# Next block's x_proj, softplus and turned u two states earlier, and z ahead of its block in a second buffer

## The chip, the cores and the metric

The kernel runs on one core of a Trainium2 chip. The metric is the device time of one execution in microseconds (us), as the median of repeated runs. The engines are TensorE (PE; its weight loads are shown as PEld), VectorE (DVE), ScalarE (ACT), GpSimd (POOL) and SyncE (SP, which issues the DMAs). Each works through its own queue in order, and semaphores tie the queues together.

## The reference, cut to what matters

The program is four layers behind one another: a selective state space layer, a mixture of experts, a linear attention with a feed-forward part, and two layers of windowed attention. Only the first is touched. It computes, for `x` of 4 x 1024 x 256 that has been layer-normalised:

```python
xz = einsum('bld,ed->ble', x, W_in);  u, z = split(xz, 2)     # 512 channels each
uc = silu(depthwise_conv3(u) + conv_b)
x_dbl = einsum('blh,eh->ble', uc, W_xproj)                    # 96 columns: dt 64, B 16, C 16
dt = softplus(einsum('blr,hr->blh', dtp, W_dt) + b_dt)
A = -exp(A_log)                                               # 16 states
def step(h, inp):                                             # over time
    h = exp(dt_t * A) * h + B_t * u_t                         # 16 states x 512 channels
    y_t = einsum('bn,bnh->bh', C_t, h)
y = (ys + D * uc) * silu(z)
out = x + einsum('blh,dh->bld', y, W_out)
```

All arithmetic is in float32.

## The kernel before, in words

`state_space_stage` cuts the 4096 tokens into N = 8 blocks of 512 (two to a sequence) and goes over NS = 16 states in each. One iteration `i` stands for one state of one block: block k = i // 16, state i % 16. Every engine has the same loop over `i` from FIRST = -20 to END, and each step of a block's preparation and of its closing is put at a fixed offset r = i - 16 k from the block's first state. So r = -12 is state 4 of the block before, r = -1 is its state 15, and the order on each engine is written out by hand. In the prologue (negative i) the first block's preparation runs with no scans beside it.

What one state takes, with the names that the profile shows:

- GpSimd `scale_u(i)` (L322): four instructions, u turned to time-major (`uT`) times the state's column of B (in `bcT`), into `ub`. `add_odd` (L336): two sums into `acc`.
- TensorE `inject` (L830): turns `ub` back to channel-major in the four banks `pu`, 16 transposes. `transpose_state` (L842): turns the scanned state of the iteration before into `pt`, 16 transposes.
- ScalarE `step_decay` (L450): exp(dt * A) into `da`, in two instructions. `weigh` (L462): two multiplications of turned states by C.
- VectorE `scan` (L620): four scans, one for each 128 channels. `add_even` (L630): two sums into `acc`.

In TensorE's queue the transposes and injections of a state stand in the order T0 T1, I0, I1, T2 T3, I2, I3, and `first_product` and `second_product`, each in two parts, put the matmuls of other blocks between them. They all use the two PSUM banks `pf`, one after the other, so every user waits for the one before.

The preparation of block k before the change, by r:

- r = -17 normalisation on ScalarE (`normalised`, L472); -19 its statistics on VectorE (L535); -18 `norm_factors` on GpSimd
- r = -12, -11 `product_u` (L687); -11, -10 `convolve` (L563) on VectorE
- r = -8 Silu of `uc` on ScalarE (L485), at the end of the iteration
- r = -6 `product_xd` (x_proj, L712), -5 to -3 `product_dt` (L734) and `magnitude` (L385, L386), -3 Exp (L488), -2 Ln (L491), -1 the sum `dt` = relu + ln on VectorE (L591, after the second scan)
- r = -3 to -1 `transpose_u` (L743) and `turn_u` (L380), which make `uT`
- r = 6, 7 `product_z` (L700) and `copy_z`; r = 8 Silu of `z` (L494)
- r = 18 to 20 `transpose_sum` (L763) and `gate` (L570); 24, 25 `product_out` (L774); 25, 26 `output` (L576)

Both Silus fall into iteration 8 of a block (z of this block, `uc` of the next), with a table load before them and one back to the Exp and Ln set behind (L521).

At the turn to the next block the order is another one. On GpSimd `scale_u` of state 0 is issued in iteration 15, not 14, and of state 1 behind the sums. On ScalarE `step_decay` of state 0 stands behind `first_product`. On TensorE all of state 0's injections stand behind `transpose_state` and `second_product` of iteration 15. `scale_u` of state 0 waits for all four `turn_u` of its block, the last of which is at r = -1. `begin_sum` (L328, four instructions, `skip` times `uT`) starts the next block's sums at r = -1 and 0.

Of the kernel before, what the change touches and what calls it, by code (L numbers as in the profile page):

```python
# [162 lines left out]
def state_space_stage(nc, tag, w, src, dst, ident):  # L163
# [6 lines left out]
    with ExitStack() as ctx:  # L170
# [17 lines left out]
        z = s.sb("z", [P, CT, BLK])  # L188
# [51 lines left out]
        FIRST, END = -20, NS * N + 11  # L240
# [51 lines left out]
        def _(pool):  # L292
# [46 lines left out]
            for i in range(FIRST, END):  # L339
                turn_ends = (i + 1) % NS == 0  # L340
                if turn_ends and 0 <= i + 1 < N * NS:
                    scale_u(i + 1)
                if not turn_ends and (i + 2) % NS and 0 <= i + 2 < N * NS:
                    scale_u(i + 2)
# [3 lines left out]
                if turn_ends and 0 <= i + 2 < N * NS:  # L348
                    scale_u(i + 2)
# [13 lines left out]
        def _(act):  # L363
            give_credit(act, weighed)

            def copy_z(k, c):
                act.wait_ge(z_made.sem, z_made.at(k, c + 1))
                nc.scalar.activation(z[:, c, :], pf[c % 2][:, :], ACT.Copy).then_inc(z_copied.sem, 1)
# [40 lines left out]
            def first_product(i):  # L409
                for k in range(N):  # L410
# [5 lines left out]
                    elif r in (-12, -11):  # L416
                        copy_u(k, 2 * (r + 12))
                    elif r in (-5, -4, -3):
                        magnitude(k, (0, 1, 3)[r + 5])
                    elif r in (-2, -1):  # L420
                        turn_u(k, 2 * r + 5)
                    elif r in (6, 7):
                        copy_z(k, 2 * (r - 6))

            def second_product(i):
                for k in range(N):
# [5 lines left out]
                    elif r in (-12, -11):  # L432
                        copy_u(k, 2 * (r + 12) + 1)
                    elif r == -6:
                        projected(k)
                    elif r == -5:
                        bc_columns(k)
                    elif r == -4:
                        magnitude(k, 2)
                    elif r in (-3, -2):  # L440
                        turn_u(k, 2 * (r + 3))
                    elif r in (6, 7):
                        copy_z(k, 2 * (r - 6) + 1)
# [32 lines left out]
            def rest_of_step(i):  # L476
                for k in range(N):
# [5 lines left out]
                    elif r == -8:  # L483
                        act.wait_ge(conv_steps.sem, conv_steps.at(k))
                        nc.scalar.activation(uc[:, :, :], uc[:, :, :], ACT.Silu).then_inc(uc_ready.sem, 1)  # L485
                    elif r == -3:
                        act.wait_ge(abs_ready.sem, abs_ready.at(k))
                        nc.scalar.activation(work[:, :, :], work[:, :, :], ACT.Exp, scale=-1.0).then_inc(soft_steps.sem, 1)  # L488
                    elif r == -2:
                        act.wait_ge(soft_steps.sem, soft_steps.at(k, 1))  # L490
                        nc.scalar.activation(work[:, :, :], work[:, :, :], ACT.Ln, bias=1.0).then_inc(soft_steps.sem, 1)  # L491
                    elif r == 8:
                        act.wait_ge(z_copied.sem, z_copied.at(k))
                        nc.scalar.activation(z[:, :, :], z[:, :, :], ACT.Silu).then_inc(z_ready.sem, 1)  # L494

            for i in range(FIRST, END):
# [9 lines left out]
                if (i + 1) % NS and 0 <= i + 1 < N * NS:  # L506
# [4 lines left out]
                if (i + 1) % NS and 0 <= i + 1 < N * NS:  # L511
# [12 lines left out]
        def _(dve):  # L524
# [41 lines left out]
            def gate(k, c):  # L566
# [3 lines left out]
                nc.vector.tensor_tensor(gatedT[:, c, :], pf[c % 2][:, :], z[:, c, :], ALU.mult).then_inc(gated_ready.sem, 1)  # L570
# [8 lines left out]
            def after_second_scan(i):  # L579
                for k in range(N):  # L580
# [3 lines left out]
                    elif r == 26:  # L584
# [3 lines left out]
                    elif r == -1:  # L588
# [5 lines left out]
            def rest_of_step(i):  # L594
                for k in range(N):
# [9 lines left out]
                    elif r == 25:  # L605
# [44 lines left out]
        def _(pe):  # L650
            give_credit(pe, bu_made, state_turned, turned_made)

            def transpose_hidden(k, d):
                if d == 0:
                    pe.wait_ge(h0_ready.sem, h0_ready.at(k))
                if k:
                    pe.wait_ge(uT_ready.sem, uT_ready.at(k - 1, 4 - d))
# [47 lines left out]
            def product_xd(k, c):  # L705
                if c == 0:
# [3 lines left out]
                    elif k:  # L710
                        pe.wait_ge(z_copied.sem, z_copied.at(0, 3))
# [4 lines left out]
            def transpose_bc(k):  # L716
# [3 lines left out]
                elif k:  # L720
                    pe.wait_ge(z_copied.sem, z_copied.at(0))
# [24 lines left out]
            def transpose_sum(k, c):  # L746
# [7 lines left out]
                elif k == N - 2:  # L754
                    pe.wait_ge(uT_ready.sem, uT_ready.at(k + 1, 4 - c))
# [10 lines left out]
            def product_out(k, half, t, part):  # L766
                if t == 0 and part == 0:
                    if half == 0:
                        pe.wait_ge(gated_ready.sem, gated_ready.at(k))
                    if k + 1 < N:  # L770
                        pe.wait_ge(z_copied.sem, z_copied.at(k + 1, 3 + half))
# [1740 lines left out]
```

## Time and profile before

| | us |
|---|---|
| median of 3 runs | 3998.52 |
| the runs | 3998.52, 3992.69, 4001.32 |
| the profiled execution's time | 3997.76 |
| its span, first to last instruction | 3995.9 |
| first scan starts, last scan ends | 66.3, 1020.2 |
| mean granted TensorE clock, share of full | 0.961 |

The scans of the state space stage take 953.9 of the 3995.9 us; what follows them is not edited. A step below is the time from the first scan of one state to the first scan of the next. In an even block a step in which VectorE never waits and has nothing else to do takes 5.76 us, in an odd block 6.00, since there the scans take a carry.

### The profile page before, as it was taken

To read this page: it belongs to the slowest core of one execution; us is meant where nothing else is said; L and a number is where in the kernel's file an instruction comes from. 1 tells how busy PE (TensorE), PEld (TensorE's weight loads), DVE (VectorE), ACT (ScalarE), POOL (GpSimd) and SP (SyncE) were. 2 spreads that over 40 slices of the span, in tenths; PEclk is the share of its full clock that TensorE was granted. 3 is DMA by queue.
4 is the path that set the end of the run, shared out by engine and by line. 5 is a ranking of instruction groups with operands and counts; after the bars stand their busy time and mean duration, and the time that the engine had idled before them with its cause. 6 is when DMAs were issued, how large, how long until landed. Compare 5 with 4: busy or idle time off the path is not lost. (4 is left out here: it accounts for less than half of the span.)

```text
span 3995.9 us, 59179 instructions
## 1 busy us (share of the span) xinstructions
PE 3643.4 (91%) x21704; PEld 2593.4 (65%) x21704; DVE 2522.0 (63%) x5386; ACT 1601.5 (40%) x3052; POOL 1392.0 (35%) x1567
## 2 busy tenths in 40 slices
PE   6888878887799999999998998999979989999799
PEld 3666666666455688888886664666645556666465
DVE  4898988899566455555554444777743357777333
ACT  5666666666100122222221213666631146666211
POOL 4778777788100000000000223444411134444111
PEclk8899999999899999999998998999989999999899
DMA  1000000000200100000001112111122011111221
GB/s 39 1 11 12 1 11 11 11 6 6 87 32 32 35 12 12 12 12 12 11 11 55 64 63 64 38 34 37 38 63 64 27 59 33 38 34 34 74 64 37
DMA packets 150197, 129.32 MB, mean 32 GB/s; under 512 B 20804, under 2 KB 147544, under 8 KB 149656
## 3 DMA queue, kind: packets, MB, share of 16 engines
q1 hardware_dynamic: 149912, 125.54, 10.0%
q8 instruction: 177, 2.90, 0.3%
q14 instruction: 108, 0.88, 0.1%
HBM read 87.73 MB, written 37.77 MB: 31 GB/s over the span
## 5 line engine op out<-in xcount | busy, mean ns | idle before, releaser
L830 PEld LDWEIGHTS ssm_pu<-ident,ssm_ub 128*128 128x128 f32 x2048 | 255.8, 150 | 220.3 <-issue 86.0
L830 PE MATMUL ssm_pu<-ident,ssm_ub 128*128 128x128 f32 x2048 | 325.4, 292 | 80.4 <-POOL ssm_ub L322 47.2
L322 POOL TENSOR_SCALAR ssm_ub<-ssm_uT,ssm_bcT 128x512 f32<-128x512 f32 x512 | 356.4, 718 | 96.7 <-ACT ssm_uT L380 63.4
L336 POOL TENSOR_TENSOR ssm_acc<-ssm_acc,ssm_weighted 128x512 f32<-128x512 f32 x256 | 328.4, 1292 | 143.4 <-ACT ssm_weighted L462 143.0
L842 PE MATMUL ssm_pt<-ident,ssm_state 128*128 128x128 f32 x2048 | 288.5, 285 | 82.6 <-DVE ssm_acc L630 58.6
L2256 PE MATMUL win_pa<-win_w_wqkv,win_hT 128*128 128x512 f32 x768 | 357.9, 603 | 1.6 <-ACT win_hT L2043 1.1
L620 DVE TENSOR_TENSOR_SCAN ssm_state<-ssm_da,ssm_carry,ssm_pu 128x512 f32<-128x512 f32 x256 | 312.2, 1260 | 21.2 <-PE ssm_pu L830 16.4
L1838 PE MATMUL glu_up<-glu_hT,glu_w_w 128*128 128x512 f32 x704 | 309.4, 599 | 3.4 <-DVE glu_hT L1761 3.4
L620 DVE TENSOR_TENSOR_SCAN ssm_state<-ssm_da,ssm_pu 128x512 f32<-128x512 f32 x256 | 296.6, 1199 | 25.1 <-PE ssm_pu L830 16.9
L842 PEld LDWEIGHTS ssm_pt<-ident,ssm_state 128*128 128x128 f32 x2048 | 240.4, 147 | 107.9 <-DVE ssm_acc L630 67.8
L2017 POOL TENSOR_TENSOR win_rotated<-win_straight,win_turned 128x512 f32<-128x512 f32 x128 | 163.0, 1274 | 417.0 <-DVE win_turned L2132 417.0
L462 ACT ACTIVATE ssm_weighted<-ssm_pt,ssm_bcT 128x512 f32<-128x512 f32 x256 | 175.7, 686 | 319.6 <-PE ssm_pt L842 273.0
L2063 ACT ACTIVATE win_probs<-win_sc,win_nbias,win_rn 128x256 f32<-128x256 f32 x512 | 281.9, 560 | 28.9 <-DVE win_nbias L2160 21.9
L450 ACT ACTIVATE ssm_da<-ssm_dt,ssm_decay 128x1024 f32<-128x1024 f32 x256 | 292.7, 1147 | 1.4 <-DVE ssm_dt L591 1.4
L2155 DVE CUSTOM_DVE_ANT_0 win_sc<-win_sc,win_c_masks 128x256 f32<-128x256 f32 x512 | 205.7, 444 | 118.2 <-PE win_sc L2273 118.2
L1273 POOL TENSOR_TENSOR lin_rstd<-lin_mv,lin_eps 128x1 f32<-128x1 f32 x32 | 6.1, 190 | 718.2 <-DVE lin_mv L142 718.2
L1473 PE MATMUL lin_pa<-lin_hT,lin_wqk 128*128 128x128 f32 x2048 | 245.7, 278 | 3.7 <-DVE lin_hT L1362 0.8
L1838 PEld LDWEIGHTS glu_up<-glu_hT,glu_w_w 128*128 128x128 f32 x704 | 135.3, 193 | 168.3 <-issue 162.4
L1473 PEld LDWEIGHTS lin_pa<-lin_hT,lin_wqk 128*128 128x128 f32 x2048 | 233.5, 192 | 13.7 <-DVE lin_qkT L1372 8.9
L1774 DVE SCALAR_TENSOR_TENSOR glu_act<-glu_up,glu_w_b,glu_gel 128x512 f32<-128x512 f32 x96 | 71.9, 749 | 252.8 <-ACT glu_gel L1731 236.6
L1117 PE MATMUL moe_ex<-moe_w_experts,moe_hT 128*128 128x512 f32 x512 | 226.0, 594 | 0.0
L2256 PEld LDWEIGHTS win_pa<-win_w_wqkv,win_hT 128*128 128x128 f32 x768 | 138.6, 194 | 131.6 <-issue 129.7
(241 smaller groups left out, 7295.3 us busy)
## 6 DMA issues: line engine op xcount, KB each, us to landing
win_raw<-in_tables SPq DMA_DIRECT2D x64, 128.0 KB, 2.2
a<-win_y SPq DMA_DIRECT2D x64, 128.0 KB, 1.7
glu_xs<-a SPq DMA_DIRECT2D x32, 256.0 KB, 3.3
glu_x<-a SPq DMA_DIRECT2D x16, 512.0 KB, 5.3
ssm_x<-in_L_attn_x SPq DMA_DIRECT2D x8, 512.0 KB, 3.9
x<-ssm_out SPq DMA_DIRECT2D x16, 256.0 KB, 2.1
moe_x<-x SPq DMA_DIRECT2D x8, 512.0 KB, 3.9
x<-moe_y SPq DMA_DIRECT2D x8, 512.0 KB, 2.9
```

Of the source, the lines that this page charges most:

```text
L322: nc.gpsimd.tensor_scalar(ub[:, i % 2, t, :], uT[:, k % 2, t, :], bcT[:, k % 2, t, n:n + 1], 1.0, ALU.mult, ALU.mult).then_inc(ub_ready.se ...
L336: nc.gpsimd.tensor_tensor(acc[:, k % 2, t, :], acc[:, k % 2, t, :], weighted[:, j, :], ALU.add)\
L450: nc.scalar.activation(da[:, i % 2, pairs[p], :], dt[:, k % 2, pairs[p], :], ACT.Exp, scale=decay[:, n:n + 1]).then_inc(da_ready.sem, 1)
L620: nc.vector.tensor_tensor_scan(state[:, i % 2, c, :], da[:, i % 2, c, :], pu[c][:, :], carry[:, n, c:c + 1] if k % 2 else 0.0, ALU.mult, A ...
L830: last = nc.tensor.transpose(pu[c][:, t * P:(t + 1) * P], ub[:, i % 2, t, c * P:(c + 1) * P], ident)
L842: last = nc.tensor.transpose(pt[t % 2][:, c * P:(c + 1) * P], state[:, i % 2, c, t * P:(t + 1) * P], ident)
L1117: last = nc.tensor.matmul(ex[pair][:, :], hT[:, turn.side, k, t * P:(t + 1) * P], experts[:, k, pair * 2 * D:(pair + 1) * 2 * D], start=(k ...
L1473: last = nc.tensor.matmul(pa[g % 2][:, r * P:(r + 1) * P], wqk[:, g // 2, k, cols], hT[:, k, :], start=(k == 0), stop=(k == KD - 1))
L1838: last = nc.tensor.matmul(bank[:, :], w1[:, k, at:at + P], hT[:, k, :], start=(k == 0), stop=(k == KD - 1))
L2063: nc.scalar.activation(probs[:, head, :], sc[j][:, r, :], ACT.Exp, bias=nbias[:, g, j, r:r + 1], scale=rn[:, turn.side, 0, head:head + 1], ...
L2155: return nc.vector.tensor_tensor_reduce(sc[j][:, r, :], sc[j][:, r, :], mask, 1.0, -3e38, ALU.add, ALU.max, highest[:, g, j, r:r + 1])
L2256: last = nc.tensor.matmul(bank[:, :], hT[:, k, :], wqkv[:, k, g * INNER:(g + 1) * INNER], start=(k == 0), stop=(k == KD - 1))
```

## The change

The preparation from x_proj to the sum of dt and the turned u moves from r = -6 ... -1 to r = -8 ... -3. The Silu of `uc` moves from -8 to -9 and that of `z` from 8 to 7, so that both are in iteration 7, and x_proj is in the iteration right behind. `product_z` and `copy_z` move from r = 6, 7 to r = -2, -1, that is into iterations 14 and 15 of the block before, for which `z` gets a second buffer. `product_out` and `output` move two iterations up. The special order at the turn is taken out on GpSimd, ScalarE and TensorE: state 0 of a block is treated as any other. The waits on the banks `pf` follow the new order. No instruction is added or dropped, and none of the DMAs is edited.

```diff
-        z = s.sb("z", [P, CT, BLK])
+        z = s.sb("z", [P, 2, CT, BLK])
-        FIRST, END = -20, NS * N + 11
+        FIRST, END = -20, NS * N + 9
@@ GpSimd, main loop @@
-                turn_ends = (i + 1) % NS == 0
-                if turn_ends and 0 <= i + 1 < N * NS:
-                    scale_u(i + 1)
-                if not turn_ends and (i + 2) % NS and 0 <= i + 2 < N * NS:
+                if 0 <= i + 2 < N * NS:
                     scale_u(i + 2)
                 if 0 <= i - 1 < N * NS:
                     add_odd(i - 1, 0)
                     add_odd(i - 1, 1)
-                if turn_ends and 0 <= i + 2 < N * NS:
-                    scale_u(i + 2)
@@ ScalarE, first_product @@
-                    elif r in (-5, -4, -3):
-                        magnitude(k, (0, 1, 3)[r + 5])
+                    elif r in (-7, -6, -5):
+                        magnitude(k, (0, 1, 3)[r + 7])
+                    elif r in (-4, -3):
+                        turn_u(k, 2 * r + 9)
                     elif r in (-2, -1):
-                        turn_u(k, 2 * r + 5)
-                    elif r in (6, 7):
-                        copy_z(k, 2 * (r - 6))
+                        copy_z(k, 2 * (r + 2))
@@ ScalarE, rest_of_step: Silu of uc, Exp, Ln, Silu of z @@
-                    elif r == -8:
+                    elif r == -9:
...
-                    elif r == -3:
+                    elif r == -5:
...
-                    elif r == -2:
+                    elif r == -4:
...
-                    elif r == 8:
+                    elif r == 7:
@@ ScalarE, main loop @@
                 first_product(i)
-                if (i + 1) % NS == 0 and 0 <= i + 1 < N * NS:
-                    step_decay(i + 1, 0)
-                    step_decay(i + 1, 1)
                 rest_of_step(i)
-                if i % NS == NS // 2:
+                if i % NS == NS // 2 - 1:
                     nc.scalar.preload_act_table_set("natural_log_exp_and_others")
@@ VectorE: output, half 1; the sum of dt; output, half 0 @@
-                    elif r == 26:
+                    elif r == 24:
...
-                    elif r == -1:
+                    elif r == -3:
...
-                    elif r == 25:
+                    elif r == 23:
@@ TensorE, product_z, the bank that it waits for @@
-                    elif k + 1 < N:
-                        pe.wait_ge(u_copied.sem, u_copied.at(k + 1, c + 3))
                     else:
-                        pe.wait_ge(gated_ready.sem, gated_ready.at(k - 1, c + 3))
+                        pe.wait_ge(uT_ready.sem, uT_ready.at(k, 4 - c))
@@ TensorE, first_product; second_product alike @@
-                    elif r == -6:
+                    elif r == -8:
                         product_xd(k, part)
-                    elif r in (-5, -4, -3) and part:
-                        product_dt(k, (0, 1, 3)[r + 5])
-                    elif r in (-2, -1) and part == 0:
-                        transpose_u(k, 2 * r + 5)
-                    elif r in (6, 7):
-                        product_z(k, 2 * (r - 6), part)
+                    elif r in (-7, -6, -5) and part:
+                        product_dt(k, (0, 1, 3)[r + 7])
+                    elif r in (-4, -3) and part == 0:
+                        transpose_u(k, 2 * r + 9)
+                    elif r in (-2, -1):
+                        product_z(k, 2 * (r + 2), part)
                     elif r in (18, 19) and part:
                         transpose_sum(k, 2 * (r - 18))
-                    elif r in (24, 25):
-                        product_out(k, 0, r - 24, part)
+                    elif r in (22, 23):
+                        product_out(k, 0, r - 22, part)
@@ TensorE, main loop @@
                 first_product(i, 0)
-                if ahead and not turn_ends:
+                if ahead:
                     inject(i + 1, 0)
...
                 second_product(i, 0)
-                if ahead and turn_ends:
-                    inject(i + 1, 0)
-                    inject(i + 1, 1)
                 if ahead:
                     inject(i + 1, 2)
```

## Rows read from the trace of the kernel before

**Rows 1.** Windows by block: length, busy PE, PEld, DVE, ACT, POOL, clock, DMA

```profile
304.76:426.82 122.06, 100.44 (x638) 78.17 (x637) 108.84 (x123) 82.95 (x119) 93.73 (x106) 0.93 0.03 10
...
sum 953.86, PE 787.64 PEld 612.59 DVE 866.33 ACT 634.07 POOL 735.10; mean PE 98.46 PEld 76.57 DVE 108.29 ACT 79.26 POOL 91.89
```

**Rows 2.** Windows by stage: blocks 1 and 2, steps 0-2, 8-11, 12-14, 15

```profile
180.34:201.94 21.60, 20.22 (x143) 19.20 (x142) 18.94 (x19) 12.31 (x19) 21.60 (x25) 0.81 0.00 1
...
241.43:272.36 30.93, 27.79 (x172) 22.26 (x170) 25.92 (x27) 19.98 (x22) 22.16 (x25) 0.94 0.11 34
...
292.18:304.77 12.59, 4.84 (x28) 4.08 (x27) 8.29 (x9) 7.70 (x12) 5.96 (x11) 0.72 0.00 1
304.77:326.42 21.65, 17.53 (x123) 16.20 (x122) 18.21 (x20) 11.55 (x18) 21.65 (x25) 0.85 0.00 1
...
364.63:395.28 30.65, 27.41 (x178) 21.79 (x176) 25.17 (x27) 21.66 (x28) 23.12 (x25) 1.00 0.11 35
395.28:414.76 19.48, 17.14 (x123) 13.36 (x122) 19.34 (x30) 18.80 (x29) 13.83 (x15) 1.00 0.01 1
414.76:426.80 12.04, 4.41 (x28) 3.67 (x27) 8.04 (x9) 7.79 (x13) 6.07 (x11) 0.74 0.00 0
```

**Rows 3.** Timeline of the turn from block 1 to block 2: start, length, instruction

```profile
291.51 1.91 ACT L491 ACTIVATE ssm_work<-ssm_work 128x2048 f32<-128x2048 f32 x1
...
294.54 2.27 DVE L591 TENSOR_TENSOR ssm_dt<-ssm_dt,ssm_work 128x2048 f32<-128x2048 f32 x1
...
297.52 1.93 PE L842 MATMUL ssm_pt<-ident,ssm_state 128*128 128x128 f32 x8 [3.61 <-DVE ssm_acc L630]
...
300.07 0.59 ACT L380 ACTIVATE ssm_uT<-ssm_pf 128x512 f32<-128x512 f32 x1
...
300.76 2.70 POOL L322 TENSOR_SCALAR ssm_ub<-ssm_uT,ssm_bcT 128x512 f32<-128x512 f32 x4 [6.55 <-ACT ssm_uT L380]
...
304.77 1.22 DVE L620 TENSOR_TENSOR_SCAN ssm_state<-ssm_da,ssm_pu 128x512 f32<-128x512 f32 x1 [4.30 <-PE ssm_pu L830]
```

**Rows 4.** Timeline of TensorE in steps 7 and 8 of block 2

```profile
359.65 1.04 PE L842 MATMUL ssm_pt<-ident,ssm_state 128*128 128x128 f32 x8
...
361.83 1.02 PE L700 MATMUL ssm_pf<-ssm_hT,ssm_w_in 128*128 128x512 f32 x2
...
363.12 1.04 PE L842 MATMUL ssm_pt<-ident,ssm_state 128*128 128x128 f32 x8
...
366.59 1.04 PE L842 MATMUL ssm_pt<-ident,ssm_state 128*128 128x128 f32 x8
```

**Rows 5.** Timeline around the two Silus, step 9 of block 2

```profile
371.14 0.69 ACT L462 ACTIVATE ssm_weighted<-ssm_pt,ssm_bcT 128x512 f32<-128x512 f32 x1 [1.27 <-PE ssm_pt L842]
...
374.96 1.90 ACT L485 ACTIVATE ssm_uc<-ssm_uc 128x2048 f32<-128x2048 f32 x1
...
376.88 1.28 ACT L521 ACT_TABLE_LOAD   x1
...
380.04 0.66 PE L842 MATMUL ssm_pt<-ident,ssm_state 128*128 128x128 f32 x4 [2.42 <-ACT ssm_weighted L462]
```

**Rows 6.** Two lines of VectorE during the scans: ns min/median/max

```profile
L563 DVE SCALAR_TENSOR_TENSOR ssm_uc<-ssm_u,ssm_conv_w,ssm_uc x56: 721/853/4276, 96.0 to 849.8; 128x512 f32<-128x512 f32 x56
...
L591 DVE TENSOR_TENSOR ssm_dt<-ssm_dt,ssm_work x8: 2254/2263/2293, 60.1 to 907.5; 128x2048 f32<-128x2048 f32 x8
```

**Rows 7.** Timeline of GpSimd and VectorE, step 5 of block 0

```profile
95.83 2.70 POOL L322 TENSOR_SCALAR ssm_ub<-ssm_uT,ssm_bcT 128x512 f32<-128x512 f32 x4
96.03 5.06 DVE L563 SCALAR_TENSOR_TENSOR ssm_uc<-ssm_u,ssm_conv_w,ssm_uc 128x512 f32<-128x512 f32 x2
...
98.48 1.27 POOL L336 TENSOR_TENSOR ssm_acc<-ssm_acc,ssm_weighted 128x512 f32<-128x512 f32 x1
```

**Rows 8.** Timeline ahead of the first scan

```profile
65.04 3.25 PE L830 MATMUL ssm_pu<-ident,ssm_ub 128*128 128x128 f32 x14 [5.21 <-POOL ssm_ub L322]
```

**Rows 9.** Window around the end of the prologue, columns as in rows 1

```profile
51.85:68.92 17.07, 10.08 (x36) 7.38 (x37) 4.92 (x4) 14.44 (x19) 7.75 (x10) 0.50 0.00 1
```

More of the change, by code:

```diff
@@ L433, in second_product @@
                         copy_u(k, 2 * (r + 12) + 1)
+                    elif r == -8:
+                        projected(k)
+                    elif r == -7:
+                        bc_columns(k)
                     elif r == -6:
[L435 to L438, printed above, removed]
                         magnitude(k, 2)
-                    elif r in (-3, -2):
-                        turn_u(k, 2 * (r + 3))
-                    elif r in (6, 7):
-                        copy_z(k, 2 * (r - 6) + 1)
+                    elif r in (-5, -4):
+                        turn_u(k, 2 * (r + 5))
+                    elif r in (-2, -1):
+                        copy_z(k, 2 * (r + 2) + 1)
             def step_decay(i, p):
@@ L505, in _ @@
                     carry_over(i - 1)
-                if (i + 1) % NS and 0 <= i + 1 < N * NS:
+                if 0 <= i + 1 < N * NS:
                     step_decay(i + 1, 0)
@@ L510, in _ @@
                 second_product(i - 1)
-                if (i + 1) % NS and 0 <= i + 1 < N * NS:
+                if 0 <= i + 1 < N * NS:
                     step_decay(i + 1, 1)
@@ L656, in transpose_hidden @@
                 if k:
-                    pe.wait_ge(uT_ready.sem, uT_ready.at(k - 1, 4 - d))
+                    pe.wait_ge(z_copied.sem, z_copied.at(k - 1, 3 + d))
                 for t in range(TB):
@@ L719, in transpose_bc @@
                     pe.wait_ge(out_ready.sem, out_ready.at(k - 2))
-                elif k:
-                    pe.wait_ge(z_copied.sem, z_copied.at(0))
                 for t in range(TB):
@@ L754, in transpose_sum @@
                 elif k == N - 2:
-                    pe.wait_ge(uT_ready.sem, uT_ready.at(k + 1, 4 - c))
+                    pe.wait_ge(z_copied.sem, z_copied.at(k + 1, 3 + c))
                 elif k % 2:
@@ L769, in product_out @@
                         pe.wait_ge(gated_ready.sem, gated_ready.at(k))
-                    if k + 1 < N:
-                        pe.wait_ge(z_copied.sem, z_copied.at(k + 1, 3 + half))
+                    if k + 2 < N:
+                        pe.wait_ge(u_copied.sem, u_copied.at(k + 2, 3 + half))
                 first = (2 * half + t) * P
@@ L809, in second_product @@
                         product_u(k, 2 * (r + 12) + 1, part)
-                    elif r == -6:
+                    elif r == -8:
                         product_xd(k, 2 + part)
-                    elif r == -5 and part == 0:
+                    elif r == -7 and part == 0:
                         transpose_bc(k)
-                    elif r == -4 and part == 0:
+                    elif r == -6 and part == 0:
                         product_dt(k, 2)
-                    elif r in (-3, -2) and part == 0:
-                        transpose_u(k, 2 * (r + 3))
-                    elif r in (6, 7):
-                        product_z(k, 2 * (r - 6) + 1, part)
+                    elif r in (-5, -4) and part == 0:
+                        transpose_u(k, 2 * (r + 5))
+                    elif r in (-2, -1):
+                        product_z(k, 2 * (r + 2) + 1, part)
                     elif r in (18, 19) and part == 0:
                         transpose_sum(k, 2 * (r - 18) + 1)
-                    elif r in (24, 25):
-                        product_out(k, 1, r - 24, part)
+                    elif r in (22, 23):
+                        product_out(k, 1, r - 22, part)
             def inject(i, c):
@@ L847, in _ @@
                     pe.wait_ge(w_in_loaded, 16)
-                elif i == -6:
+                elif i == -8:
                     pe.wait_ge(weights, 16 * 8)
@@ L853, in _ @@
                     transpose_state(i - 1, 1)
-                turn_ends = i % NS == NS - 1
                 first_product(i, 0)
-                if ahead and not turn_ends:
+                if ahead:
                     inject(i + 1, 0)
                 first_product(i, 1)
-                if ahead and not turn_ends:
+                if ahead:
                     inject(i + 1, 1)
```

11 lines of the change are left out of this document (5 added, 6 removed).

## The prediction

> **What bounds the kernel now.** I read the windows by block first. The eight blocks of scans take 953.9 us, of which VectorE is busy 866.3; GpSimd has 735.1 [rows 1]. VectorE sets the pace, and the stage can win no more than its idle 87.5 us. The reader should hold every edit against that number.
>
> Then the windows by stage, to see where that idle time lies [rows 2]. In steps 12 to 14 of block 2 there is next to none (19.48 - 19.34 = 0.14); in step 15, the turn, 12.04 - 8.04 = 4.00, and 12.59 - 8.29 = 4.30 in block 1. In steps 0 to 2 it is 2.66 and 3.44. In steps 8 to 11 it is 5.01 and 5.48. These three places are 12.0 and 12.9 us a block; seven times their mean is 87 us, which is nearly all of it.
>
> Third, the timeline of the turn [rows 3]. VectorE does the sum of dt at 294.54, so TensorE, which needs `add_even` behind it, stands 3.61 us. The last quarter of turned u is copied at 300.07, GpSimd starts `scale_u` of state 0 at 300.76 after 6.55 us idle and needs 2.70, and only then can the injection begin and VectorE scan at 304.77, after 4.30 us. TensorE runs at 1.2 GHz from this hole on: eight transposes take 1.93 us at 297.52 against 1.04 at full clock [rows 3, 4].
>
> **The turn, step 15.** The change takes the chain turned u, `scale_u`, injection off the path: uT is complete in iteration 13, `scale_u` of state 0 is issued in 14, and its 2.70 us end some 4 us before the injection in 15. The 4.15 us (mean of the two blocks) go. What comes in their place:
>
> *Sum of dt in step 13.* Its VectorE time moves at no cost in itself. But it needs the Ln. Before, the Ln ended at 291.51 + 1.91 = 293.42 and the sum began at 294.54, so 1.1 us of slack [rows 3]; that slack rests on the statistics of step 13 (steps 12 to 14 of block 2 are 19.48 us against 3 x 5.76 = 17.28, so 2.2), which lay between Exp and Ln and now come behind the sum. So VectorE waits about 2.2 - 1.1 = 1.1 us. Also, GpSimd was waiting for turned u when this sum ran at the turns, and it took 2254 to 2293 ns [rows 6]. Now it has `scale_u` and `add_odd` beside it. What that can cost shows in the convolution, likewise two SBUF inputs on VectorE: 721 ns at best, 853 in the median, 4276 at worst [rows 6], the worst when it began 0.2 us behind a `scale_u` [rows 7]. So 0.1 to 3.5 us, in part under the wait for Ln. I take 1.3 for Ln and GpSimd together.
>
> The Trainium skill (SBUF — State Buffer, Who interferes with whom) says that a VectorE instruction with two SBUF inputs and a GpSimd instruction that reads SBUF exclude each other for a whole instruction, and whichever comes second is blocked. By that rule the wait would end with the GpSimd instruction in progress; rows 7 show a wait longer than any one instruction there, so the rule agrees in kind, and the sum goes by the rows.
>
> *z in steps 14 and 15.* In steps 7 and 8 z's matmuls and the output's stand between the transposes, and one state takes TensorE 366.59 - 359.65 = 6.94 us. Two z matmuls and four transposes take 363.12 - 361.83 = 1.29, so a z matmul 0.43 and eight in a step 3.44 [rows 4]. Steps 14 and 15 so want 6.94 us of TensorE against 5.76 or 6.00 of VectorE. One z pair (0.86) fits in the hole that step 13 leaves; the rest makes TensorE about 2 us late at the end of step 15, where it has roughly 2.3 before VectorE's `add_even` waits, and step 0, with only eight extra transposes, gives it back. I take 0.3. At nothing or 2.4 us lie the bounds.
>
> *Clock.* Step 13 now holds the sum and the statistics, so TensorE stands some 3.5 and then 1.5 us. After such holes the clock was 0.72 and 0.74 of full over the turn [rows 2]. If a quarter of the 6.94 us of step 14 runs at 1.2 GHz, 1.7 us of TensorE are lost, part of it in time in which it waits anyway: I take 0.7 (0 to 3.5, which is half of the step).
>
> Turn afterwards: 1.3 + 0.3 + 0.7 = 2.3. Saved 4.15 - 2.3 = 1.85, seven times: **13 us**.
>
> **Steps 0 to 2.** Mean idle 3.05 us. GpSimd is busy in all of their 21.60 and 21.65 us [rows 2]: it starts the block late (idle 6.55 at the turn, [rows 3]) and has four instructions of `begin_sum` on top. The lateness goes, `begin_sum` stays: four of 1.27 like L336 [rows 7], so 5.1 us over steps 15 and 0. A plain step is 2.70 + 2 x 1.27 = 5.24 us of GpSimd, so it regains 0.5 a step, and its lead is about 4 us (`scale_u` may begin some 7 us before it is wanted, and needs 2.70). I leave 1.4 us of waiting; saved 1.6, but less in blocks whose idle time there is shorter: seven times 1.45, **10 us** (0 to 17).
>
> **Steps 7 to 11.** Two effects of opposite sign. z leaves steps 6 and 7 and the output takes its place, so 6.94-us steps end at step 8 instead of 10. But x_proj now stands right behind the Silus. In block 2: the second transposes of step 7 end at 364.0 [rows 4], the weighting (0.69, [rows 5]) by 364.9; table load and both Silus fill the time from the weighting's end, 371.83, to 376.86 = 5.0 us [rows 5], so `uc` is ready at 369.9. TensorE is at x_proj at 366.59 + 0.87 = 367.5 [rows 4] and stands 2.4 us. Queued behind are injections of state 9 and T2, T3 of state 7; with two pairs of x_proj and two injections before them (2.6 us) T2 is done at about 373.2. VectorE, which now has an output in each of steps 7 and 8, wants it at about 371.3: 2.0 us idle. T3 needs the weighting, which after a Silu comes 380.04 - 376.86 = 3.2 us later [rows 5], about the same time. By the same walk smaller waits follow for T0 of state 8 (0.8) and for the dt products, which wait for the xd copy as before (0.8). With 0.8 for a slow stretch of clock that makes 4.4 in an even block. In an odd block each step is 0.24 longer and TensorE a microsecond less late, so the same sum gives 2.5. Mean over four even and three odd: 3.6. Saved 5.25 - 3.6 = 1.6, seven times: **11 us** (-15 to 20).
>
> **Prologue.** Here z comes without cover: 16 matmuls after the last turned u, which TensorE has done 5.21 us before 65.04, so they begin at 60 to 61; ten of them stand ahead of the first injection [rows 8]. The clock is at half in this stretch [rows 9], so a matmul takes 0.86 and ten 8.6 us: the injection begins near 69.4. At full clock it would begin near 65.4. Near the slow end, since the stretch before is slow: **4 us lost** (0.4 to 7). In the tail nothing changes: only empty iterations go. The output's and the x loads' DMAs leave two steps earlier; no wait of VectorE names a load during the scans, so nothing.
>
> **Sum.** 13 + 10 + 11 - 4 = 30 us. The profiled execution took 3997.8, within 0.02% of the median 3998.5: 3997.8 - 30 = **3968 us**.
>
> **The rivals.**
>
> *A. The clock eats the turn.* The double hole of step 13 leaves TensorE at 1.2 GHz for all of step 14, when it has most to do. Each turn then loses half of 6.94 us, less what it waits anyway: 3.3 in place of 0.7, and 30 - 7 x 2.6 = 12 us are saved, **3986 us**. For it: two holes there as now. Against: the second is shorter, since the injections of step 13 lie between.
>
> *B. No change.* GpSimd takes VectorE's place around the turn. From step 14 to 2 it has 5 x 5.24 + 5.1 = 31.3 us of its own, and the sum of dt blocks it 2.3 more, against some 29.5 of VectorE. Then the 10 us of steps 0 to 2 don't come and 1.9 more a turn is lost: 30 - 10 - 13 = 7, **3991 us**, within 0.2% (8 us) of before, which is about what a measurement here can tell. Against: over a block GpSimd is busy 93.7 of 122.1 us, so it catches up [rows 1].
>
> *C. Slower: x_proj behind the Silus.* If the burst on ScalarE begins half a step (2.9 us) later than reckoned, TensorE stands 5.3 us at x_proj, and after so long a hole half of a 6.94-us step at 1.2 GHz costs 3.5 in place of my 0.8. That is 5.6 more in each of seven blocks and 3 in the prologue: 42 us, **4010 us**. It decides from some 4.3 us a block beyond my 3.6. Against: T2 and T3 of step 7 bound the burst's start, and they are early.
>
> *D. More.* Ln in time, no slow clock: turn 1.0, steps 7 to 11 at 2.5: 9 + 8 us more, **3951 us**.
>
> **How the numbers follow.** Forecast 0.56, D 0.14, A 0.15, B 0.08, C 0.07. The forecast's own range is 3957 to 3980. To hold 8 in 10 the range takes in D and A and leaves B and C: 3948 to 3989. Faster by over 0.2% (below 3990.5): the forecast, D, nearly all of A: 0.85. Within 0.2%: B and a little of A: 0.08. Slower: C, 0.07.
>
> **What would show it.** Right: blocks of 116 to 119 us instead of 122 to 124; no VectorE wait for `pu` at the turn, `scale_u` of state 0 over before step 15; step 13 of 10 us and more, with L591 over 2.3 us where it meets GpSimd; a TensorE wait of 2 to 3 us for L485 at L712; first scan near 70. Wrong: a wait for L712 over 4 us, step 14 or 15 over 8 us at half clock, or L336 holding L462 in steps 0 to 2 as before.

## The result, and the profile after

The changed kernel takes **3943.04 us** (median of 4 runs, 3941.39 to 3943.43) beside 3998.18 (4 runs) for the kernel before: a ratio of 0.9863, 95% interval 0.9846 to 0.988. It is 55 us faster, where 30 were forecast; the time lies 5 us under the low end of the range, 3948. The profiled execution has a span of 3941.6 us (3995.9 before), and its scans take 896.9 us (953.9 before).

Windows by block of the changed kernel (blocks 0 to 2, then the sum over all eight), columns as in [rows 1]:

```profile
68.51:179.54 111.03, 93.42 (x580) 69.67 (x579) 104.27 (x114) 81.72 (x117) 93.77 (x104) 0.94 0.00 1
179.54:295.48 115.94, 100.31 (x657) 76.15 (x656) 111.81 (x121) 82.01 (x108) 96.83 (x107) 0.99 0.03 10
295.48:408.74 113.26, 98.18 (x637) 75.79 (x636) 108.53 (x123) 82.45 (x118) 95.55 (x105) 0.97 0.03 10
...
sum 896.95, PE 770.09 PEld 590.55 DVE 863.75 ACT 633.07 POOL 752.29; mean PE 96.26 PEld 73.82 DVE 107.97 ACT 79.13 POOL 94.04
```

Blocks 1 to 5 are 113.2 to 116.0 us long instead of the 116 to 119 that I expected. VectorE's idle time in the scans, 87.5 us before [rows 1], is 33.2. GpSimd's busy time is longer by 17 us (752.3 against 735.1) in scans that are shorter by 57. Two rows of VectorE's waits from 66 to 960 us (us in total, times, longest), the first of the kernel before, the second of the changed one, show the chain that left the turn; the one wait that stays is the first scan's:

```profile
DVE ssm_state L620 <- PE ssm_pu L830: 33.2, 8, 4.5
```

```profile
DVE ssm_state L612 <- PE ssm_pu L816: 4.2, 1, 4.2
```

Windows by stage (block 1: steps 0-2; block 2: steps 0-2, 12-14, 15, and behind these steps 13 and 14 by themselves), columns as in [rows 2]:

```profile
179.54:198.51 18.97, 18.16 (x145) 15.56 (x144) 18.70 (x20) 15.61 (x26) 18.96 (x22) 1.00 0.01 1
...
295.48:313.45 17.97, 15.74 (x124) 13.23 (x123) 17.97 (x20) 14.45 (x24) 17.97 (x20) 1.00 0.01 1
...
379.97:402.98 23.01, 17.90 (x118) 14.16 (x116) 21.87 (x30) 17.91 (x26) 18.52 (x19) 0.93 0.00 1
402.98:408.74 5.76, 5.76 (x36) 4.14 (x35) 5.76 (x7) 3.34 (x5) 5.68 (x10) 1.00 0.01 3
...
385.73:397.24 11.51, 8.07 (x54) 7.12 (x53) 10.37 (x18) 8.92 (x14) 10.17 (x11) 0.85 0.00 1
397.24:402.98 5.74, 5.16 (x28) 3.15 (x27) 5.74 (x8) 3.23 (x6) 3.35 (x4) 1.00 0.00 0
```

The turn is now a plain step: 5.76 us with VectorE busy throughout, where it was 12.04 with 4.00 idle [rows 2]. Steps 0 to 2 went from 21.65 to 17.97 us with no idle time, though GpSimd is still busy in all of them. Steps 12 to 14 are longer, since the sum of dt lies there now; 1.14 us of idle time came with it. The granted clock was 0.72 over the turn to block 2 and 0.85 in its steps 0 to 2 before [rows 2]; now it is 1.00 in both, and 0.85 in step 13 of block 2.

The table has VectorE's idle time (length of a step less VectorE's busy time in it) over all eight blocks, by stage, in us; the kernels below the first two are the experiments.

| kernel | 0-2 | 3-6 | 7-11 | 12 | 13-14 | 15 | idle | busy | scans |
|---|---|---|---|---|---|---|---|---|---|
| before | 19.5 | 1.0 | 35.9 | 0 | 0.9 | 30.3 | 87.5 | 866.3 | 953.9 |
| **after** | 1.3 | 1.0 | 24.9 | 0 | 5.2 | 0.8 | 33.2 | 863.7 | 896.9 |
| turn_order_back | 13.5 | 1.0 | 23.6 | 0 | 5.3 | 6.2 | 49.6 | 867.3 | 916.9 |
| gpsimd_order_back | 19.3 | 1.0 | 26.1 | 0 | 5.4 | 18.8 | 70.6 | 870.3 | 940.9 |
| pe_act_order_back | 1.6 | 1.0 | 22.3 | 0 | 5.1 | 6.1 | 36.1 | 862.9 | 899.0 |
| before_no_begin | 5.2 | 1.0 | 36.0 | 0 | 0.9 | 28.8 | 71.8 | 863.6 | 935.4 |
| after_double_begin | 41.7 | 1.0 | 22.5 | 0 | 5.1 | 0.9 | 71.2 | 868.9 | 940.1 |
| stats_early | 3.0 | 1.0 | 23.9 | 0.9 | 1.1 | 3.8 | 33.7 | 862.4 | 896.2 |
| narrow_z | 4.4 | 1.0 | 25.9 | 0 | 5.1 | 0 | 36.5 | 866.2 | 902.7 |
| silu_uc_first | 2.3 | 1.0 | 17.3 | 0 | 5.2 | 0.9 | 26.6 | 863.3 | 889.9 |
| weigh_first | 1.3 | 1.0 | 24.4 | 0 | 5.1 | 0.9 | 32.7 | 863.8 | 896.5 |
| silu_and_weigh | 2.0 | 1.0 | 9.2 | 0 | 5.2 | 0.5 | 17.8 | 862.2 | 880.0 |
| all_three | 3.0 | 1.0 | 9.3 | 0.9 | 2.5 | 5.1 | 21.9 | 863.8 | 885.7 |

From before to after: steps 13 to 15 -25.2, steps 0 to 2 -18.1, steps 7 to 11 -11.0, VectorE's busy time -2.6, the start of the first scan +2.2 (68.51 against 66.3), after the last scan +0.4. Together -54.3, which is by what the spans differ.

Timeline of step 13 of block 2, the place to which the sum of dt moved, and of what follows (start, length, instruction):

```profile
387.07 1.94 ACT L486 ACTIVATE ssm_work<-ssm_work 128x2048 f32<-128x2048 f32 x1
...
388.06 4.74 POOL L322 TENSOR_SCALAR ssm_ub<-ssm_uT,ssm_bcT 128x512 f32<-128x512 f32 x4
...
389.04 2.52 DVE L583 TENSOR_TENSOR ssm_dt<-ssm_dt,ssm_work 128x2048 f32<-128x2048 f32 x1 [0.99 <-ACT ssm_work L486]
...
392.28 1.09 PE L828 MATMUL ssm_pt<-ident,ssm_state 128*128 128x128 f32 x8 [3.40 <-DVE ssm_acc L622]
...
395.42 1.70 PE L828 MATMUL ssm_pt<-ident,ssm_state 128*128 128x128 f32 x8
395.83 2.70 POOL L322 TENSOR_SCALAR ssm_ub<-ssm_uT,ssm_bcT 128x512 f32<-128x512 f32 x4 [0.38 <-PE ssm_pu L816]
```

Three things are to be seen. The sum waits 0.99 us for the Ln, as worked out (1.1). It runs beside `scale_u` and takes 2.52 us, only 0.25 more than before [rows 6]; the price fell on `scale_u`, 4.74 us instead of 2.70: one of its four instructions took 2.73 us, the others 0.70. At all seven turns it is so, and seven times 2.04 are 14 of the 17 us by which GpSimd's busy time grew (an estimate). And `scale_u` of the next block's state 0, the one at 395.83, is over at 398.5, some 10 us before that state's first scan at 408.74. TensorE stands 3.40 us behind the sum, does eight transposes at full clock (1.09 us) and then eight in 1.70 us, where 1.04 is the full clock and 1.93 the half one [rows 3, 4]. So the half clock came, but in step 13 (0.85) and not in step 14 (1.00), where I had put it, and VectorE has no idle time in steps 14 and 15.

### The profile page after: what moved, and what is told of

It reads as the page before. It is cut to its first block and busy times, and to the rows that moved or that the text cites. A ratio compares the mean times of both kernels' runs of the same rounds, so it can differ in the third digit from the quotient of the medians.

```text
span 3941.6 us, 59176 instructions
## 1 busy us (share of the span) xinstructions
PE 3632.8 (92%) x21704; PEld 2572.8 (65%) x21704; DVE 2520.7 (64%) x5386; ACT 1600.2 (41%) x3052; POOL 1410.5 (36%) x1567
## 5 line engine op out<-in xcount | busy, mean ns | idle before, releaser
L322 POOL TENSOR_SCALAR ssm_ub<-ssm_uT,ssm_bcT 128x512 f32<-128x512 f32 x512 | 371.7, 747 | 65.6 <-ACT ssm_uT L375 41.9
L816 PEld LDWEIGHTS ssm_pu<-ident,ssm_ub 128*128 128x128 f32 x2048 | 241.1, 144 | 183.0 <-issue 76.6
L816 PE MATMUL ssm_pu<-ident,ssm_ub 128*128 128x128 f32 x2048 | 315.2, 282 | 42.8 <-DVE ssm_state L612 29.0
```

The costliest lines, as they stand in the source:

```text
L322: nc.gpsimd.tensor_scalar(ub[:, i % 2, t, :], uT[:, k % 2, t, :], bcT[:, k % 2, t, n:n + 1], 1.0, ALU.mult, ALU.mult).then_inc(ub_ready.se ...
L816: last = nc.tensor.transpose(pu[c][:, t * P:(t + 1) * P], ub[:, i % 2, t, c * P:(c + 1) * P], ident)
```

## The experiments

All ratios are to the kernel before, run on the same chip, with 95% intervals. The medians are to be held against 3943.0 for the changed kernel. The kernel before had medians of 3995.6 to 3998.2 in the four sets of runs, so a difference of 2 or 3 us between medians of two sets says nothing.

### Which part of the turn matters

**turn_order_back**: the changed kernel with the old order at the turn on three engines.

```diff
@@ GpSimd @@
-                if 0 <= i + 2 < N * NS:
+                if turn_ends and 0 <= i + 1 < N * NS:
+                    scale_u(i + 1)
+                if not turn_ends and (i + 2) % NS and 0 <= i + 2 < N * NS:
                     scale_u(i + 2)
...
+                if turn_ends and 0 <= i + 2 < N * NS:
+                    scale_u(i + 2)
@@ ScalarE: step_decay of state 0 behind first_product @@
@@ TensorE: inject(i + 1, 0) and (i + 1, 1) behind second_product(i, 0) @@
```

> The changed kernel with the old order at the turn put back on GpSimd, ScalarE and TensorE: state 0's scale_u in iteration 15, its decay behind first_product, its injections behind T2, T3. Preparation and z stay early. Theory 1 (turned u was late; with it early, the order matters little): VectorE's idle time in step 15 is 1 us or less a turn instead of 0.1, the kernel 0 to 7 us slower than the changed one (3943). Theory 2 (the order itself held VectorE: state 0's injections wait behind T2, T3 and z): 2 to 4 us a turn come back in step 15 and some of the 2.8 us a block in steps 0 to 2, so 20 to 35 us slower, 3963 to 3978.

3965.26 us, 0.9919 [0.9905, 0.9934]. So 22 us of the 55 hang on the order, once the preparation is early, and the other 33 come without it. No run has the new order with the old preparation. Most of what comes back is not at the turn (6.2 against 0.8), where theory 2 had 2 to 4 us a turn, but in steps 0 to 2 (13.5 against 1.3). Of the 20 us by which the scans are longer, 3.6 are busy time of VectorE, nearly all of it in step 5 of block 0 (what happens there is told with narrow_z).

**gpsimd_order_back** and **pe_act_order_back**: the same edit in two halves, GpSimd's alone, and TensorE's with ScalarE's.

> The changed kernel with the old order at the turn on GpSimd alone: scale_u of state 0 in iteration 15, that of state 1 behind the sums. The whole old order came out 20 us of scans slower than the changed kernel (916.9 against 896.9 us), 12 of them as idle time in steps 0 to 2. Theory 1 (GpSimd's start an iteration late is what costs): 15 to 20 us slower than the changed kernel, with most of the idle time in steps 0 to 2. Theory 2 (the injections behind z and the transposes on TensorE cost): 5 us or less.

> The changed kernel with the old order at the turn on TensorE and ScalarE alone. Theory 1 (GpSimd's order costs): 3 to 6 us slower than the changed kernel, the 5.4 us of step 15, and little in steps 0 to 2. Theory 2 (TensorE's order costs): 15 to 20 us, as the whole old order.

GpSimd's half: 3986.01 us, 0.9974 [0.9964, 0.9984]. The other half: 3944.81 us, 0.987 [0.9857, 0.9884]. Windows over all scans, first of GpSimd's half, then of the other (columns as in [rows 1]):

```profile
68.23:1009.17 940.94, 778.05 (x5004) 601.54 (x5002) 870.34 (x932) 633.32 (x856) 752.86 (x824) 0.96 0.03 8
```

```profile
71.19:970.18 898.99, 764.97 (x4997) 588.92 (x4994) 862.90 (x932) 632.79 (x856) 751.56 (x821) 0.97 0.03 8
```

With GpSimd's busy time as after (752.9 against 752.3), the scans are 44 us longer when GpSimd alone has the old order (37.4 of idle time, 6.6 of VectorE's busy time), where I expected 15 to 20, and 2 us longer with the other half. Timeline at the turn from block 1 to 2 in GpSimd's half:

```profile
302.85 2.71 POOL L322 TENSOR_SCALAR ssm_ub<-ssm_uT,ssm_bcT 128x512 f32<-128x512 f32 x4
...
305.61 1.09 PE L821 MATMUL ssm_pu<-ident,ssm_ub 128*128 128x128 f32 x4 [2.23 <-POOL ssm_ub L322]
...
309.78 0.75 DVE L627 SCALAR_TENSOR_TENSOR ssm_acc<-ssm_pt,ssm_bcT,ssm_acc 128x512 f32<-128x512 f32 x1 [3.52 <-PE ssm_pt L833]
```

Turned u has long been there, but `scale_u` is issued an iteration late; TensorE, whose injection now stands ahead of the transposes, waits 2.23 us for it, and VectorE 3.52 for the transposes queued behind. The old orders belong together: all three cost 20 us, GpSimd's alone 44. That TensorE's order is what softens it in turn_order_back follows from the queue and the two halves; no run shows it apart from ScalarE's part. What ScalarE's late decay costs can be read from the waits of the second half: VectorE waits for it ahead of the first scan (6.2 us) and at each of the seven turns, 5.8 us in all, which is nearly all of its 6.1 in step 15. The row of the waits (us in total, times, longest):

```profile
DVE ssm_state L615 <- ACT ssm_da L445: 12.0, 8, 6.2
```

**stats_early**: the statistics one iteration up, away from the sum of dt.

```diff
-                    if r == -19:
+                    if r == -20:
                         statistics(k)
```

> The changed kernel with the statistics of the block after next one step earlier, in step 12 (r = -20), between Exp and Ln as they stood before the change. Theory 1 (the wait for Ln in step 13 comes from the statistics moving behind the sum of dt): the wait of 1.0 us in even blocks goes, 4 to 5 us in all, 3938 to 3940, and the hole of TensorE in step 13 is shorter. Theory 2 (the wait comes from ScalarE's own load): the wait stays, no difference.

3941.64 us, 0.986 [0.9844, 0.9876]: not to be told from 3943.0, and short of the 3938 to 3940 expected. The wait for the Ln goes (steps 13 and 14: 5.2 to 1.1) but 3.0 us come up in step 15, 1.7 in steps 0 to 2 and 0.9 in step 12. Statistics and Ln are tied as I said. What brings the new idle time was not sought.

### GpSimd's lead in steps 0 to 2

Two explanations were open for the idle time there before: GpSimd's late start alone, or that start with `begin_sum` on top. A third is TensorE's half clock, which in the kernel before reached from the turn into step 0.

**before_no_begin**: the kernel before, `begin_sum` on one column of 512. **after_double_begin**: the changed kernel, each `begin_sum` instruction twice.

```diff
-  nc.gpsimd.tensor_tensor(acc[:, k % 2, t, :], uT[:, k % 2, t, :], skip[:, :], ALU.mult)
+  nc.gpsimd.tensor_tensor(acc[:, k % 2, t, 0:1], uT[:, k % 2, t, 0:1], skip[:, 0:1], ALU.mult)
@@ the other kernel @@
+  nc.gpsimd.tensor_tensor(acc[:, k % 2, t, :], uT[:, k % 2, t, :], skip[:, :], ALU.mult).then_inc(begun_once, 1)
+  pool.wait_ge(begun_once, k * TB + t + 1)
   nc.gpsimd.tensor_tensor(acc[:, k % 2, t, :], uT[:, k % 2, t, :], skip[:, :], ALU.mult).then_inc(begun.sem, 1)
```

> The kernel before, with begin_sum cut to one column of each of its four instructions (skip times u is left out but for that column; acc is cleared once at the start). GpSimd loses about 4 us of work a block, all of it next to the turn. Theory 1 (the idle time of steps 0 to 2 comes from GpSimd starting late at the turn): most of the 19.5 us there stay, 14 or more. Theory 2 (it comes from begin_sum on top of the late start): 5 us or less are left there, and the kernel is 13 to 18 us faster than before, 3980 to 3985.

> The changed kernel with every begin_sum instruction issued twice, 5.1 us more of GpSimd a block over steps 15 and 0. My prediction's lead of about 4 us, used up by one begin_sum, would give 4 to 5 us more idle time of VectorE a block, 28 to 35 us, 3971 to 3978. If the lead with its slack behind it is longer than supposed, 1 to 2.5 us a block, 7 to 17 us, 3950 to 3960.

before_no_begin: 3980.22 us, 0.9957 [0.9942, 0.9972]. after_double_begin: 3988.36 us, 0.9978 [0.9969, 0.9988]. Windows over all scans of the two:

```profile
67.06:1002.48 935.42, 780.43 (x5014) 602.16 (x5012) 863.63 (x932) 635.93 (x855) 705.64 (x824) 0.95 0.02 8
```

```profile
68.12:1008.18 940.06, 777.91 (x5004) 605.93 (x5002) 868.86 (x932) 632.53 (x857) 789.43 (x855) 0.95 0.02 8
```

Before, taking `begin_sum` out (29 us of GpSimd) took the idle time of steps 0 to 2 from 19.5 to 5.2: it needed both, the late start and `begin_sum`. The turn kept its idle time (28.8 us) and its stretch at half clock, so that stretch alone doesn't make the idle time of steps 0 to 2; whether slow stretches within these steps lengthened it was not tried. After, with the one `begin_sum` in place, 1.3 us are idle; a second one adds 37 us to GpSimd's busy time and 40 us of idle time in steps 0 to 2, about one for one, and 45 us to the median, where 28 to 35 were expected. So the changed kernel stands close to an edge: GpSimd's lead covers one `begin_sum` and little or nothing beyond it. Smaller additions, which would show where the edge lies, were not run. Timeline in the doubled kernel, behind the turn to block 3, and a row of its waits from 66 to 960 us:

```profile
434.75 1.09 PE L819 MATMUL ssm_pu<-ident,ssm_ub 128*128 128x128 f32 x8 [1.47 <-POOL ssm_ub L323]
...
439.77 0.75 DVE L625 SCALAR_TENSOR_TENSOR ssm_acc<-ssm_pt,ssm_bcT,ssm_acc 128x512 f32<-128x512 f32 x1 [2.73 <-POOL ssm_acc L331]
...
DVE ssm_acc L625 <- POOL ssm_acc L331: 21.6, 8, 3.1
```

TensorE waits for `ub`, and `add_even` on VectorE for `begin_sum` itself (L331), without which it has nothing to add to: GpSimd is the bound there. That direct wait is 21.6 of the 40 us. It was 3.0 in all in the kernel before, and the changed one has none. So a late `scale_u` is only one of the two ways in which GpSimd holds VectorE.

### The Silus and x_proj, steps 7 to 11

Timeline of the changed kernel, step 8 of block 2:

```profile
355.07 1.89 ACT L480 ACTIVATE ssm_uc<-ssm_uc 128x2048 f32<-128x2048 f32 x1
...
357.01 1.10 PE L700 MATMUL ssm_pf<-ssm_uc,ssm_w_x 128*96 128x512 f32 x2 [2.32 <-ACT ssm_uc L480]
...
359.43 0.67 ACT L457 ACTIVATE ssm_weighted<-ssm_pt,ssm_bcT 128x512 f32<-128x512 f32 x1
...
360.39 0.75 DVE L622 SCALAR_TENSOR_TENSOR ssm_acc<-ssm_pt,ssm_bcT,ssm_acc 128x512 f32<-128x512 f32 x1 [2.04 <-PE ssm_pt L828]
```

x_proj waits 2.32 us for the Silu (2.4 were worked out), and VectorE 2.04 (2.0). Three runs ask which of two things costs: z's Silu ahead of uc's, or the table load and the decay ahead of the weighting.

```diff
@@ silu_uc_first: ScalarE, rest_of_step @@
-                for k in range(N):
+                for k in reversed(range(N)):
@@ weigh_first: ScalarE, the iteration behind the Silus @@
+                back = i % NS == NS // 2 and i > 0
+                if back and 0 <= i - 1 < N * NS:
+                    weigh(i - 1, 0)
+                if back:
+                    nc.scalar.preload_act_table_set("natural_log_exp_and_others")
                 if 0 <= i + 1 < N * NS:
                     step_decay(i + 1, 0)
-                if 0 <= i - 1 < N * NS:
+                if not back and 0 <= i - 1 < N * NS:
                     weigh(i - 1, 0)
...
-                if i % NS == NS // 2 - 1:
+                if i == NS // 2 - 1 - NS:
                     nc.scalar.preload_act_table_set("natural_log_exp_and_others")
```

> The changed kernel with the Silu of uc ahead of the Silu of z in iteration 7, so that x_proj can start 1.9 us earlier. Theory 1 (my prediction: VectorE's idle time in step 8 comes from x_proj's wait for Silu, 2.3 us on TensorE): 1.5 to 1.9 us less a block, 10 to 13 us in all, 3930 to 3933. Theory 2 (the whole burst on ScalarE holds the weighting, and T3 behind it, so TensorE only waits at T3 instead of at x_proj): step 8 shorter, step 9 longer by the same, 0 to 3 us in all, 3940 to 3943.

> The changed kernel with, behind the two Silus, the weighting of state 7 ahead of the table load and the decay of state 9, so that T3 is free 2.4 us earlier. Silu order as in the changed kernel. Theory 1 (x_proj's wait is what costs): nothing, 3942 to 3944. Theory 2 (T3 is what costs): T3 2.3 us earlier, steps 8 and 9 together 1.5 to 2 us shorter a block, 10 to 14 us in all, 3929 to 3933.

> Both of the last two edits together. Theory 1 (x_proj's wait alone): as with the Silu order alone. Theory 2 (a chain with x_proj's wait and T3's, one behind the other): steps 8 and 9 2 to 3 us shorter a block than in the changed kernel, until the decay of state 9 at the end of the burst is the bound: 14 to 20 us in all, 3923 to 3929.

silu_uc_first: 3936.75 us, 0.9851 [0.9835, 0.9867], between its two theories. weigh_first: 3943.46 us, 0.9865 [0.985, 0.988], no gain. Both: **3927.14 us**, 0.9825 [0.9811, 0.984], which is 16 us faster than the changed kernel. Timeline of silu_uc_first, where the first wait is short and the second takes its place:

```profile
351.75 1.10 PE L700 MATMUL ssm_pf<-ssm_uc,ssm_w_x 128*96 128x512 f32 x2 [0.52 <-ACT ssm_uc L480]
...
356.68 0.66 PE L828 MATMUL ssm_pt<-ident,ssm_state 128*128 128x128 f32 x4 [1.67 <-ACT ssm_weighted L457]
...
357.54 2.33 DVE L612 TENSOR_TENSOR_SCAN ssm_state<-ssm_da,ssm_pu 128x512 f32<-128x512 f32 x2 [1.16 <-PE ssm_pt L828]
```

And of silu_and_weigh, at the end of ScalarE's burst:

```profile
348.97 0.67 ACT L457 ACTIVATE ssm_weighted<-ssm_pt,ssm_bcT 128x512 f32<-128x512 f32 x1
349.66 1.28 ACT L505 ACT_TABLE_LOAD   x1
...
352.13 2.33 DVE L617 TENSOR_TENSOR_SCAN ssm_state<-ssm_da,ssm_pu 128x512 f32<-128x512 f32 x2 [0.64 <-ACT ssm_da L445]
```

The two waits lie one behind the other in TensorE's queue. Cutting the second alone is worth nothing, since x_proj still holds the queue; cutting the first alone is worth 7.6 us of the 24.9; cutting both 15.7. The weighting runs right behind the Silus, ahead of the table load, and the decay, now behind it, costs VectorE 0.64 us.

### z's matmuls, and all together

**narrow_z**: z's matmuls on one column of 512. They still take 17.2 us of TensorE in the scans (60.5 in the changed kernel), so the run prices about 43 us of z, not all of it.

```diff
-  nc.tensor.matmul(pf[c % 2][:, :], w_in[...], hT[:, k % 2, d, 0:BLK],
+  nc.tensor.matmul(pf[c % 2][:, 0:1], w_in[...], hT[:, k % 2, d, 0:1],
```

> The changed kernel with each z matmul cut to one column (the other 511 columns of z are then what the bank held before, so z is left out). The instructions and waits stay. It prices z's 6.9 us of TensorE a block. If z in steps 14 and 15 is covered: only the prologue gains, first scan at about 66.3 instead of 68.5 and 1 us behind it, 2 to 4 us in all, 3939 to 3941. If z delays VectorE at the turn as my 0.3 us a turn has it: 2 us more.

3943.73 us, 0.9866 [0.9851, 0.9881]: no gain, where 2 to 4 us were expected. Windows over all scans:

```profile
65.40:968.12 902.72, 753.76 (x5003) 595.23 (x5002) 866.24 (x932) 632.53 (x856) 752.47 (x827) 0.96 0.03 8
```

The first scan starts at 65.4, so z costs 3.1 us in the prologue. In steps 13 to 15 its absence is worth 0.8 us in all eight blocks. But the scans are 5.8 us longer. 3.1 of that is idle time in steps 0 to 2, 1.0 in steps 7 to 11, and 2.5 busy time of VectorE, which is one long convolution instruction in step 5 of block 0, as one row of narrow_z shows (ns min, median, max):

```profile
L555 DVE SCALAR_TENSOR_TENSOR ssm_uc<-ssm_u,ssm_conv_w,ssm_uc x64: 717/853/4772, 31.1 to 807.0; 128x512 f32<-128x512 f32 x64
```

against this in the changed kernel:

```profile
L555 DVE SCALAR_TENSOR_TENSOR ssm_uc<-ssm_u,ssm_conv_w,ssm_uc x64: 715/858/1739, 30.7 to 803.1; 128x512 f32<-128x512 f32 x64
```

**all_three**: silu_and_weigh and stats_early together.

> The changed kernel with the Silu of uc first, the weighting ahead of the table load, and the statistics in step 12. The first two gave 17 us of scans. The statistics alone took the wait for Ln (5.2 us to 1.1) and gave nothing, as 3 us more came in step 15. If that wait in step 15 has a cause of its own, the three give what the two give, 3924 to 3929; if it came from ScalarE's burst, 3 to 4 us more, 3920 to 3924. Either beats both kernels.

3931.02 us, 0.9834 [0.9821, 0.9848], no better than silu_and_weigh and above the 3924 to 3929 expected: steps 7 to 11 keep their gain (9.3), the idle time of steps 13 and 14 goes in part (2.5), and step 15 has 5.1 us. silu_and_weigh has the lowest median of these; the intervals of the two overlap.

## Why the prediction was wrong in its size

**Direction and mechanism** were right: VectorE set the pace, the three places named held its idle time, and the chain turned u, `scale_u`, injection left the path. What failed are two terms of the sum, the turn (13 us for a measured 25.2) and steps 0 to 2 (10 for 18.1): in both, the idle time that I left in place was not there. The range did not reach as far as their own bounds together.

**"Turn afterwards: 1.3 + 0.3 + 0.7 = 2.3", thirteen saved: failed.** Measured is 0.85 us a turn (steps 13 to 15), 25 us saved. Of its three parts:
- Ln and GpSimd, 1.3: the Ln's wait is 0.99, and there are four of them, in even blocks, not seven (the chain of waits: 4 times, 4.0 us). In an odd block, with scans 0.24 us a step longer, the sum doesn't wait for the Ln; that the longer scans are the reason is not shown. GpSimd's part is 0.25 in VectorE's busy time. I took the cost to be VectorE's; it fell on `scale_u`, which had the room.
- z, 0.3: narrow_z shows 0.8 us in eight blocks, 0.1 each, for the 7/10 of z that it takes out.
- Clock, 0.7: the half clock came (0.93 of full in steps 12 to 14, [rows 2] had 1.00), but at the end of step 13 (0.85), not in the long step 14 (1.00), and VectorE's idle time in steps 14 and 15 is 0.8 us over all blocks. The term was put a step too late.

**"I leave 1.4 us of waiting" in steps 0 to 2, ten saved: failed.** Measured is 1.3 us over all blocks, 18.1 saved, just past my bound of 17. The bound itself was nearly the answer: I had worked out that GpSimd's lead (about 4 us and 0.5 a step) nearly covers 5.1 us of `begin_sum`, and then left half of the idle time for caution, with no row for it. before_no_begin and gpsimd_order_back show the two causes, and after_double_begin that the edge is near: 37 us more of GpSimd work, some 4.6 a block, lose 40.

**Steps 7 to 11, 11 us: right in size**, 11.0, and the two waits of step 8 came as walked through, but the sum is right in part by luck. I had 4.4 us left in an even block and 2.5 in an odd one. Block 2 has 3.46 (2.04 in step 8 and 1.42 in step 9), since its granted clock is 1.00 there and the 0.8 for a slow stretch did not come; block 1, an odd one, has 3.52, with a clock of 0.81 in step 8. Over the seven blocks these errors cancel (3.5 a block against 3.6). The 11.0 also hold 1.3 us of block 7, which I had not counted, and the seven blocks had 4.9 us each before, not 5.25. What I didn't see is that a good part of what I forecast to remain could be had by order alone.

**Prologue, +4: right in sign**, 2.2 measured, as the timeline ahead of the first scan shows:

```profile
61.14 6.80 PE L690 MATMUL ssm_pf<-ssm_hT,ssm_w_in 128*128 128x512 f32 x10 [1.29 <-ACT ssm_uT L375]
...
67.78 0.60 PE L816 MATMUL ssm_pu<-ident,ssm_ub 128*128 128x128 f32 x4
...
68.51 7.23 DVE L612 TENSOR_TENSOR_SCAN ssm_state<-ssm_da,ssm_pu 128x512 f32<-128x512 f32 x6 [4.23 <-PE ssm_pu L816]
```

Ten z matmuls took 6.8 us: 8.6 were reckoned at 1.2 GHz throughout and 4.3 would do at full clock, so the clock rose within them. z costs 3.1 us here (narrow_z), more than the 2.2 by which the first scan is later; what gives the other 0.9 back was not sought.

**VectorE's busy time, not in the sum**: -2.6 us. The convolution's longest instruction fell from 4276 ns [rows 6] to 1739: step 5 of block 0 now meets GpSimd at another moment (9.28 us instead of 12.44). narrow_z shows it come back with no edit near it (13.60), so it is worth some 4 us of luck either way.

**The range.** Rival D, "more", was put at 3951 and took the turn down to 1.0, but kept 1.4 in steps 0 to 2. With the turn and the prologue about as measured (turn 0.9: 3.25 x 7 = 23; prologue 2), my own upper bound for steps 0 to 2 (17) and steps 7 to 11 as forecast (11), the sum is 49 us and 3949. The other 5 us are 2.2 more in steps 13 to 15, 1.1 more in steps 0 to 2 and 2.6 of busy time, less 0.6 in the prologue and behind the scans. Rivals A, B and C are refuted: no turn lost to the clock, scans not bound by GpSimd (one `begin_sum` more brings the time to 3988.4, near B's 3991), and x_proj's wait 2.3 to 2.9 us, 16.8 over seven blocks, far from 5.3.

## What to carry to other kernels

When a chain is taken off the path, ask of each queue how much lead it then has over the work that it faces: where the sum says that the lead just covers it, take the wait as gone and name the edge, rather than leave half of it; in the one case run beyond the edge, a microsecond of work cost about one. When two waits lie behind one another in one in-order queue, an edit to either may show little; try both before either is given up.

## What the runs showed of the hardware

- A VectorE sum of two SBUF inputs beside GpSimd's `scale_u` costs VectorE 0.25 us (2.52 against 2.26) and GpSimd 2.04 (4.74 against 2.70). In block 2 the sum begins 0.98 us behind the first of four `scale_u` instructions, within the second, and the third takes 2.73 us instead of 0.70. The Trainium skill (SBUF — State Buffer, Who interferes with whom) says that order decides who blocks; this row agrees, the next ones do not in full.
- The other way round, one VectorE instruction can stand through several of GpSimd's: the convolution took 4.28 us before and 4.77 in narrow_z, against 0.72 at best. Before, it began within the first of four `scale_u` [rows 7]; in narrow_z it began within an `add_odd`, 0.26 us ahead of the first of four `scale_u` (2.74 in all). In both it ended about 0.55 us behind the end of the `add_odd` that follows, though three or four of the `scale_u` had begun after it. Why it waited for several in a row, where the sum waited for one at most, is not shown. The wait shows as busy time, so an idle-time count misses it.
- With z's TensorE work cut by 43 us (PE's whole busy time fell by less, from 770.1 to 753.8), the mean granted clock over the scans fell, from 0.97 to 0.96, and VectorE's scans took 5.8 us longer. There are additional stretches at 1.2 GHz at step 14 in five blocks, in step 2 of blocks 2 and 6, and from the prologue into steps 0 and 1 of block 0. The idle time of steps 0 to 2 in narrow_z (4.4 us) lies mostly in blocks 0, 2 and 6, in steps with such a stretch (3.9); that the clock is its cause was not tried on its own.
